# Moving the last two tiles of each norm from VectorE to GpSimdE in a fused FFN, state-space and FFN block

## What is computed

```python
x = x + 0.5 * ffn(layernorm(x), W1, b1, W2, b2)
x = x + ssm(layernorm(x), Wi, bi, conv_w, conv_b, Wdt, bdt, A_log, Bm, Cm, Dv, Wo, bo)
x = x + 0.5 * ffn(layernorm(x), W1, b1, W2, b2)
# ffn: eight groups of 512 tokens, each with its own weights; no activation between its two products
# ssm: 512 inner channels, 16 states each, a skip connection x * Dv.mean() at its end
h = h * exp(dt_t * A) + dt_t * Bm * u_t       # one step of the scan over time, for each channel and state
```

## Time and profile before

| | |
|---|---|
| median of 3 runs | 786.12 us (785.98 to 790.87) |
| the profiled execution | 788.75 us |
| its span in the trace | 786.9 us |
| busy: PE, DVE, ACT, POOL | 645.0, 673.5, 602.0, 305.1 us |
| first scan begins, last scan ends | 49.6, 761.8 us |
| scans on VectorE | 288, 584.8 us |

### The profile page before, as it was taken

One profiled execution on the slowest core, in us unless ns is written; L12 is line 12 of the kernel. 1 busy time (PEld: TensorE's weight loads), 2 busy tenths in 40 slices (PEclk: granted clock), 3 DMA queues, 4 the chain that ended last, 5 costly groups with the idle time before them and its releaser, 6 DMA issues.

```text
span 786.9 us, 8285 instructions
## 1 busy us (share of the span) xinstructions
PE 645.0 (82%) x2912; PEld 332.3 (42%) x2912; DVE 673.5 (86%) x460; ACT 602.0 (76%) x1066; POOL 305.1 (39%) x188
## 2 busy tenths in 40 slices
PE   7857686979984999998886999995768998756967
PEld 5632332633441465544241574541213644312636
DVE  2437847699999998999999998999999999999680
ACT  2488858689887789989786999898788697673453
POOL 0107530134284756626457742729900054000030
PEclk9997887999998999999997999997978998986979
DMA  8342344270738060162736060434152513532001
GB/s 298 129 160 68 120 142 167 95 252 20 296 122 304 9 234 8 61 233 98 250 110 237 10 232 1 182 112 192 50 178 64 195 47 119 176 121 93 1 1 53
DMA packets 40010, 103.08 MB, mean 131 GB/s; under 512 B 4064, under 2 KB 13024, under 8 KB 39968
## 3 DMA queue, kind: packets, MB, share of 16 engines
q1 hardware_dynamic: 37408, 94.40, 32.8%
q10 hardware_dynamic: 2560, 8.14, 4.5%
HBM read 23.08 MB, written 4.19 MB: 35 GB/s over the span
## 4 chain that ended last, share of the span: by engine, by line
PE 33%; issue 25%; ACT 19%; POOL 14%; DMA 6%; DVE 3%; ACTq 1%; POOLq 0%; SPq 0%; DVEq 0%
ACT G L1052 7%; PE Y L1328 6%; PE MB L1295 5%; DMA XI<-XI 5%; PE MB L1352 5%; POOL MS L838 4%; PE MB L1254 3%; PE MB L1213 3%; PE MB L1273 3%; POOL X L831 3%; ACT XN L879 2%; DVE G L1172 2%; POOL XN L817 2%; ACT XI L972 2%; POOL LV L800 2%
## 5 line engine op out<-in xcount | busy, mean ns | idle before, releaser
L1052 ACT ACTIVATE G<-RD,COL 128x1024 f32<-128x1024 f32 (+1 forms) x288 | 279.7, 1042 | 88.0 <-PE Y L1328 84.3
L1172 DVE TENSOR_TENSOR_SCAN G<-G,STT,RV 128x1024 f32<-128x1024 f32 (+1 forms) x160 | 314.3, 2023 | 12.1 <-ACT G L1052 11.6
L1172 DVE TENSOR_TENSOR_SCAN G<-G,RV 128x1024 f32<-128x1024 f32 (+1 forms) x128 | 270.5, 2168 | 10.9 <-ACT G L1052 5.9
L1328 PE MATMUL Y<-G,RW 128*32 128x512 f32 x1024 | 140.7, 666 | 57.7 <-DVE G L1172 53.9
L791 POOL TENSOR_SCALAR LV<-LV 128x4 f32<-128x4 f32 x19 | 18.9, 996 | 318.4 <-ACT XN L879 318.1
L1295 PE MATMUL MB<-XI,DIAG 128*64 128x512 f32 x248 | 73.1, 724 | 29.1 <-DMA XI<-XI 29.1
L1328 PEld LDWEIGHTS Y<-G,RW 128*32 128x32 f32 x1024 | 27.7, 115 | 142.4 <-DVE G L1172 75.5
L831 POOL TENSOR_SCALAR X<-X,LV 128x256 f32<-128x256 f32 x32 | 86.8, 2722 | 0.8
L800 POOL TENSOR_TENSOR LV<-LV,HALF 128x4 f32<-128x4 f32 x24 | 49.2, 2051 | 64.9 <-DVE LV L1127 63.4
L1254 PE MATMUL MB<-MT,XF 128*128 128x256 f32 x256 | 63.6, 393 | 9.2 <-ACT XF L899 7.2
L838 POOL TENSOR_SCALAR MS<-MS,MV 128x256 f32<-128x256 f32 x12 | 34.9, 2912 | 79.5 <-DVE MV L1106 79.5
(11 more groups left out here) (88 smaller groups left out, 761.6 us busy)
## 6 DMA issues: line engine op xcount, KB each, us to landing
RD<-DW SPq DMA_DIRECT2D x60, 512.0 KB, 3.6
RV<-DW SPq DMA_DIRECT2D x60, 512.0 KB, 6.0
W<-in_w SPq DMA_DIRECT2D x48, 256.5 KB, 3.4
XI<-XI ACTq DMA_DIRECT2D x30, 256.5 KB, 5.6
X<-in_x SPq DMA_DIRECT2D x8, 512.0 KB, 5.7
out<-X SPq DMA_DIRECT2D x8, 512.0 KB, 3.0
G<-in_w SPq DMA_DIRECT2D x4, 513.0 KB, 8.7
RV<-in_w SPq DMA_DIRECT2D x4, 513.0 KB, 12.6
```

The lines of the kernel that those rows point to most:

```text
L1052: eng.activation(G[:, i % NG, t0:t1], RD[:, q, t0:t1], ACT.Exp, scale=NAC[:, states(i):states(i) + 1]).then_inc(sems["exp"])
L1172: eng.tensor_tensor_scan(g, g, RV[:, (4 * k + q) % NR, t0:t1], STT[:, idx:idx + 1] if goes_on else 0.0, ALU.mult, ALU.add).then_inc(sems[" ...
L1328: ins = eng.matmul(Y[32 * q:32 * q + 32, 512 * h:512 * h + 512], RW[:, states(i + o), :], G[:, (i + o) % NG, 512 * h:512 * h + 512], start ...
```

## The change

1. `norm` on GpSimdE does all four tiles, and `vnorm` is gone from VectorE for all but the early norms and norm 22, whose four tiles VectorE does alone.
2. `WAIT` goes from 4 to 5; the extra place that stood behind `vnorm` is gone, so `xt` stands as far behind `norm` as before.
3. `skip` is four stages, one for each tile, each with its own semaphore count; the output projection waits for the two tiles that it reads. Its second operation is an add in place of a subtract (the sign goes into the offset).
4. `msv` multiplies by 1.0 and adds, in place of adding twice.
5. `PLAN`, `DTS` and `PROJ` name each block by itself, `RATE` is 170 in place of 200, and two of the four `repw` DMAs of a block are placed later.

```diff
-RATE, STORE = 200, 100
+RATE, STORE = 170, 100
-PLAN = {"outs": (0, 2), "back0": (0, 11), "back1": (1, 1), "x0": (0, 0), "first0": (0, 10), "front0": (0, 1),
...
+PLAN = {"outs": ((3, 3), (7, 10), (12, 3)), "back0": ((4, 3), (8, 14), (12, 11)),
...
+        "front1": ((0, 10), (4, 9), (8, 9)), "ln0": ((0, 15), (5, 6), (8, 14)),
...
-SENDS, LATE = {9: (0, 1), 12: (2,), 14: (3,)}, {14: (0, 1, 2), 15: (3,)}
+SENDS, LATE = {9: (0,), 11: (1,), 13: (2,), 14: (3,)}, {14: (0, 1, 2), 15: (3,)}
-WAIT = 4
+WAIT = 5
 def normed(c):
-    return ("vnorm",) if early(c) else ("norm", "vnorm")
+    return ("vnorm" if early(c) or c == 22 else "norm",)
@@ norm(c) in schedule()
-        if not early(c):
+        if normed(c) == ("norm",):
             do("norm", c)
         for _ in range(0 if early(c) else WAIT):
             yield 0
         if c == 22:
             yield from after(("scan", len(UNITS) - 1))
-        do("vnorm", c)
-        if not early(c):
-            yield 0
+        if normed(c) == ("vnorm",):
+            do("vnorm", c)
@@ skips(it) in schedule()
         for hf in range(2):
-            do("skip", 6 * it + 2 + hf)
-            yield 0
+            for i in range(4):
+                do("skip", 6 * it + 2 + hf, i)
+                yield 0
@@ GpSimdE, stage norm
-                    for i in (2, 3):
+                    for i in range(4):
                         ins = eng.tensor_scalar(xn[:, i, :], v[:, i, :], lv[:, 3, i:i + 1], lv[:, 4, i:i + 1],
                                                 ALU.mult, ALU.add)
@@ GpSimdE, stage skip
-                        ins = eng.tensor_scalar(v[:, i, :], v[:, i, :], lv[:, 5, i:i + 1], lv[:, 6, i:i + 1],
-                                                ALU.mult, ALU.subtract)
-                    ins.then_inc(sems["skip"])
+                    eng.tensor_scalar(v[:, i, :], v[:, i, :], lv[:, 5, i:i + 1], lv[:, 6, i:i + 1],
+                                      ALU.mult, ALU.add).then_inc(sems["skip"])
@@ GpSimdE, stage msv
-                        ins = eng.tensor_scalar(MS[:, i, 0:256], MS[:, i, 0:256], MV[:, i:i + 1], 0.0, ALU.add, ALU.add)
+                        ins = eng.tensor_scalar(MS[:, i, 0:256], MS[:, i, 0:256], 1.0, MV[:, i:i + 1], ALU.mult, ALU.add)
@@ VectorE, stage vnorm
-                    for i in range(4 if early(c) else 2):
+                    for i in range(4):
```

More of the change, by code:

```diff
@@ L244, in norm @@
         if c >= 6:
-            yield from after(("vnorm", c - 6))
+            yield from after(*((part, c - 6) for part in normed(c - 6)))
         while len(order) >= 2 and free(order[-2]) not in placed:
@@ L438, in outs @@
                 yield from after(("yz", *gated(last, pr)))
-                yield from after(("skip", 6 * it + 2 + pr // 2))
+                yield from after(("skip", 6 * it + 2 + pr // 2, 2 * (pr % 2) + 1))
                 yield 1
@@ L450, in begin @@
     def begin(k, s):
-        it, r = divmod(k, 4)
         for first, chain in ((DTS, dts), (PROJ, proj)):
-            ko = (16 * k + s - first) // 16
-            if 1 < ko < 16 and (s - first) % 16 == 0:
-                yield chain(ko)
+            for ko in range(2, 16):
+                if 16 * k + s == 16 * ko + first[ko % 4]:
+                    yield chain(ko)
             if (k, s) == (0, 8):
                 yield chain(1)
-        if it:
-            if PLAN["outs"] == (r, s):
+        for it in range(NIT):
+            if (k, s) in PLAN["outs"][it - 1:it]:
                 yield outs(it - 1, 1)
[L462 to L466, removed]
             for hf in range(2):
-                if PLAN[f"x{hf}"] == (r, s):
+                if (k, s) in PLAN[f"back{hf}"][it - 1:it]:
+                    yield back(it - 1, hf)
+            for hf in range(2):
+                if (k, s) in PLAN[f"x{hf}"][it:it + 1]:
                     yield load(2 * it + 2 + hf)
-                if PLAN[f"front{hf}"] == (r, s):
+                if (k, s) in PLAN[f"front{hf}"][it:it + 1]:
                     yield front(it + 1, hf)
             for hf in range(2):
-                if PLAN[f"ln{hf}"] == (r, s):
+                if (k, s) in PLAN[f"ln{hf}"][it:it + 1]:
                     yield norm(6 * it + 8 + hf)
[L475 to L481, removed]
+            for hf in range(2):
+                if (k, s) in PLAN[f"first{hf}"][it:it + 1]:
+                    yield merge(2 + hf)
+                if (k, s) in PLAN[f"merge{hf}"][it:it + 1]:
+                    yield merge(2 * it + 4 + hf)
+            if (k, s) in PLAN["skips"][it:it + 1]:
                 yield skips(it + 1)
-        if it == 3 and PLAN["outs3"] == (r, s):
-            yield outs(it, 0)
+        if (k, s) in PLAN["outs3"]:
+            yield outs(3, 0)
     def run(steps):
@@ L820, in do @@
                 elif stage == "skip":
-                    c, = a
+                    c, i = a
                     _, _, _, v, lv, _ = tokens(c)
```

15 lines of the change are left out of this document (7 added, 8 removed), and 5 rows, old and new, of the table PLAN.

## The result

The changed kernel takes **849.0 us** (median of 4 runs, 844.21 to 849.51) where the kernel before takes 787.18 beside it (4 runs, 785.98 to 790.87). The ratio is 1.076, with a 95% interval from 1.072 to 1.080: 62 us slower, where 29 were forecast. The side is right, and the time lies 16 us outside the range. The profiled execution took 844.21 us with a span of 842.1 and a mean granted clock of 0.885 (788.75, 786.9 and 0.914 before).

The account below looks back on a forecast made before the run. VectorE was taken as the bound, all but full from 123.5 to 715 us, with TensorE full from 254 to 344. Profiled 788.75 - 14.5 + 44 = 818.3, median 2.6 lower: 815 us forecast, range 772 to 833.

Parts of the forecast that it names:

- The tile: A norm tile on GpSimdE beside VectorE's scans was claimed to span two scans, 4.5 us, against 0.69 with VectorE idle.
- once for the scalars and once for the data: Claimed reason for two scans: GpSimdE's tile is let in between scans twice, for its two SBUF scalars and its data.
- a tile takes one scan: Rival: a norm tile on GpSimdE spans one scan, a chain is 8 scans, two norms stall; 780 us, chance 0.27.
- VectorE pays in full: Rival: each GpSimdE tile takes one scan and costs VectorE 0.6 us, 27 us in all; 798 us, chance 0.08.
- Net 14.5 us removed from VectorE: Fifteen norms' tiles leaving VectorE remove 23.5 us of work and waiting, less 9 us for scans lengthened by GpSimdE tiles.
- The stall term: Late norm tiles hold TensorE at `xt`, so VectorE starves for `exp`: eight stalls of 5.5 us, 44 us added.
- the eight stalls named: Norms 9, 12, 5, 15, 18, 11, 21, 17 starve scans 64, 96, 112, 128, 160, 176, 192, 244.
- The other edits: 0: The `skip` and `msv` edits, `repw` DMA moves and PLAN places were counted as costing or gaining 0 us.
- Nothing where no stall is: PLAN's places move by a few scans, which was claimed to cost nothing wherever VectorE does not stall.
- Nearly every norm stalls: Rival: norms pile up on GpSimdE faster than idle times clear them, 13 stalls of 5.5 us; 843 us, chance 0.1.

## Why the prediction was wrong in size

**The tile: right.** It takes 4.5 us beside scans where two scalars come from SBUF, and 2.3 where none does. The prediction's reading of why, once for the scalars and once for the data, is not borne out as it stands: one scalar from SBUF comes without a second scan (2.45 us). Why the second one brings it is open. Four tiles in a row took less than the 17.8 us of the sum, since the first is often short: 14.2 to 16.2 us in six of the seven norms that TensorE waited for, 10.2 in norm 18. The rival "a tile takes one scan" is out. So is "VectorE pays in full": the scan in which a tile ends is 0.1 us longer, where the tile alone takes 0.55. The rule of the Trainium skill that was cited there (SBUF — State Buffer, "SBUF: two separate sides"), that whoever starts first holds the port pair for its whole instruction, does not hold for VectorE in these rows. For GpSimdE the rows agree in so far as its tile waits for a scan to end; that a tile waits for two is not in that rule.

**Net 14.5 us removed from VectorE: near the measured 14.1 by luck, and wrong as a term of the sum.** The 14.5 were 13.4 of work and 10.1 of waiting, less 9 for longer scans. What fell by 14.1 is busy time alone: the tiles' group went from 24.1 to 8.3 us, over the whole run, and the scans from 584.8 to 583.7, so the 9 us aren't there. The sum took 45 tiles as new beside scans; 27 of the changed kernel's 72 tiles met scans, where 20 of 38 did before. And with none of the tiles on GpSimdE VectorE is busy for 7.6 us more at the same time of the whole: VectorE's small jobs and its waits trade against each other here.

**The stall term: right in kind, too small.** Of the eight stalls named, six are in the trace, at 6.9 (scan 96), 7.0 (112), 8.0 (160), 7.7 (176), 7.5 (192) and 5.2 us (before `yz`, in scans 240 to 255): 42.3 in all, close to the 44 of the sum, but by luck: two stalls fewer, and all but the last longer than the 5.5 us of the forecast. The missed item is TensorE's clock. The forecast took `xt` at 1.06 us and `red` at 1.92 from rows at full clock, together 2.98. In the stalls before scans 112, 160, 176 and 192 the two take 4.95, 5.13, 5.61 and 5.16 at half clock, which is 2.0 to 2.6 us more; before scan 96 `xt` and the `outs` products take some 1.8 more. Less that, the five stalls are 5.1 to 5.9 us. This is an estimate from rows of the one trace; no run holds the clock and moves the tiles. TensorE's wait at `xt` is 64.7 us in total (over 50 was forecast), ended by norms 9, 12, 5, 18, 11, 21 and 17, seven of the eight. Norms 4, 14, 19 and 20 ran through in a stall, as said. Norm 15 did not starve scan 128, and norm 9 not scan 64, since `off` fell into a short idle time.

The term also left out what stands *behind* each stall. The reading is that TensorE and ScalarE then have a backlog; the next `dt`, `w`, `yz` or `exp` is late once more: 1.4 and 1.8 us after scan 96, 2.0 at 104, 1.8 and 1.9 after 160, 2.3 at 168, 2.4 at 184, 4.7 at 200, 5.6 at 248. Not all of it comes from the stalls: the kernel with all but the tiles, which has none of the six stalls, waits 1.7 us at 168, 2.9 at 200 and 2.4 at 248. The kernel with the tiles alone, whose order is that of before, shows the term without the tables: its VectorE idles 831.0 - 660.2 = 170.8 us against 113.4, so 57 in that execution and not 44; by medians it is 49 + 14 = 63. This is a term mis-sized by 13 to 19 us.

**"The other edits: 0" was the second failure, 16 us.** The edits of skip and msv cost nothing, as said. The moves in PLAN and the tables do. The prediction had seen that msv 4 stands behind skip 8 and judged it within the slack of the `exp`; it priced the `exp` in hand and not what else stands on TensorE behind `mt`, nor that those products run at half clock after the wait. "Nothing where no stall is" was no argument: one step of `xt` costs 49 us in an order in which no GpSimdE tile is late.

Together: 19 + 16 = 35, and 849.0 - 815 is 34. "Nearly every norm stalls" gave 843, nearest in time but not in mechanism: half of the norms did not stall.

## What to carry to other kernels

Where three engines are each 76 to 86% busy in an order written out by hand, busy time taken from the fullest engine need not be a gain; ask for each move which engine waits next for its result, price what TensorE does after a long wait from rows at its lower clock, and look for a second wait behind every stall. Before work is moved to GpSimdE beside a VectorE that never pauses, count its scan ends and not its length: an operand more in SBUF can double it. And before a long study of one cause, move a harmless constant of the order by one: here one step alone cost as much as the four tiles.

## What the runs showed of the hardware

- A tile of 128x256 on GpSimdE takes 0.41 us with constants, 0.48 with one scalar from SBUF and 0.56 with two where VectorE is idle (means over the three traces). Back to back beside scans of 2.3 us it takes 2.37, 2.44 and 4.59. The step is between one and two scalars, and nothing in the idle lengths hints at it.
- After waits of 5.8 to 19.3 us for a norm's last tile TensorE was at the lower of its two clock levels, and the eight transposes of an `xt` took 1.94 to 1.97 us in place of 1.06. Sixteen matmuls of `red` took 2.98 to 3.64 us with their start in such a stretch and 1.92 outside. So in these rows the wait cost more than its own length.
- Multiply and subtract takes 1.22 us on a tile of 128x256 on GpSimdE, multiply and add 0.55 (four skip tiles in 2.16 us in the changed kernel, at 207.64). Beside scans both take about 4.6: the kernel gains nothing by the shorter form.

```profile
207.64 2.16 POOL L833 TENSOR_SCALAR X<-X,LV 128x256 f32<-128x256 f32 x4
```
